# Gated attention and mixture of experts: the dense expert behind the last tile, eight tiles loaded right behind the table

## What is computed

```python
x = x + tanh(g_xattn) * (0.6 * sigmoid(si[:, :, None] + sj[:, None, :] + b) + 0.4 * layernorm(x))
xf = layernorm(x).reshape(-1, 256)
scores = sigmoid(xf @ w_router)                 # 1024 x 32
# the 4 best of 8 groups by (scores + corr_bias), and of their experts the 6 best
combine = zeros.at[token, topk_idx].add(scores[topk_idx])
eo = einsum('etm,emh->eth', silu(xf @ gate_w[e]) * (xf @ up_w[e]), down_w)
routed = einsum('te,eth->th', combine, eo)
shared = silu(xf @ sh_gate_w) * (xf @ sh_up_w) @ sh_down_w
out = x + tanh(g_ffn) * (routed + shared)
```

## Time and profile before

| | |
|---|---|
| median of three runs | 255.59 us (254.35 to 256.19) |
| span of the profiled execution | 256.1 us, from the first to the last instruction |
| TensorE products / weight loads | 220.1 us (86%) / 172.2 us (67%) |
| VectorE / ScalarE / POOL | 130.3 (51%) / 79.8 (31%) / 147.0 (57%) us |
| tiles | 56, in 7 rounds of eight |
| mean transfer rate | 208 GB/s |

### The profile page before, as it was taken

The page is one execution under the profiler, slowest core; times in us unless marked ns, Lnnn a source line. Parts: engine busy times, 40 slices in busy tenths (PEclk is TensorE's granted clock), DMA queues, the critical chain, the costliest instruction groups (busy, mean ns, idle before and its releaser), DMA issues.

```text
span 256.1 us, 5045 instructions
## 1 busy us (share of the span) xinstructions
PE 220.1 (86%) x1043; PEld 172.2 (67%) x1044; DVE 130.3 (51%) x528; ACT 79.8 (31%) x222; POOL 147.0 (57%) x139
## 2 busy tenths in 40 slices
PE   6896899996899986999999999999999998996000
PEld 5886687884667754877787777778777776774000
DVE  2598768989545542434444534444443443443344
ACT  3607022020011222343434344344444433433000
POOL 6226557777777742564675657656575665465500
PEclk9659599999799999999999999999999999999555
DMA  6999999999999989899785658767677675357787
GB/s 194 274 295 275 408 405 332 243 327 331 320 355 337 385 230 359 179 230 238 140 144 104 114 95 161 115 117 116 103 123 107 113 109 89 42 62 139 157 215 248
DMA packets 41016, 53.32 MB, mean 208 GB/s; under 512 B 5134, under 2 KB 35438, under 8 KB 40998
## 3 DMA queue, kind: packets, MB, share of 16 engines
q1 hardware_dynamic: 24944, 30.40, 40.3%
q0 software_dynamic: 11280, 17.99, 35.5%
q10 hardware_dynamic: 4774, 4.74, 7.1%
HBM read 31.72 MB, written 21.40 MB: 207 GB/s over the span
## 4 chain that ended last, share of the span: by engine, by line
PE 69%; DVE 13%; DMA 11%; issue 3%; POOL 1%; ACTq 1%; ACT 1%; SPq 0%; POOLq 0%
PE pG L734 25%; PE pY L748 17%; PE pG L673 5%; PE pX L728 5%; DMA sum_dram<-xnT,idx 5%; PE pH L742 4%; PE pG L757 4%; DMA xg<-rows_dram 3%; PE pY L684 3%; PE pY L776 3%; DMA given<-in_L_xattn_b_dram 2%; DMA wgu<-sum_dram 2%; PE pX L614 1%; DVE xs L900 1%; DVE rows L894 1%
## 5 line engine op out<-in xcount | busy, mean ns | idle before, releaser
L435 POOL DMA_INDIRECT sum_dram<-xnT,idx x56 | 87.1, 1556 | 61.6 <-ACT xnT L549 36.3
L734 PE MATMUL pG<-wgu,sdown 128*128 x224 | 76.1, 462 | 1.6 <-issue 1.1
L423 POOL DMA_INDIRECT rows_dram<-rows,row_i x48 | 47.2, 983 | 19.0 <-issue 13.8
L748 PE MATMUL pY<-wd,sup 88*128 x224 | 57.5, 379 | 0.0
L1122 DVE COPY sup<-pH 88x256 f32<-88x256 f32 x56 | 23.5, 420 | 58.0 <-PE pH L742 58.0
L734 PEld LDWEIGHTS pG<-wgu,sdown 128*128 128x128 f32 x224 | 38.4, 191 | 14.6 <-issue 2.6
L549 ACT ACTIVATE xnT<-pY,wt 128x256 f32<-128x256 f32 x56 | 26.6, 474 | 57.2 <-PE pY L748 24.7
L748 PEld LDWEIGHTS pY<-wd,sup 88*128 88x128 f32 x224 | 38.0, 190 | 3.2 <-issue 0.2
L742 PEld LDWEIGHTS pH<-ident,sgate 128*88 128x88 f32 x112 | 17.8, 161 | 13.6 <-issue 0.5
L542 ACT ACTIVATE sgate<-pG 128x176 f32<-128x176 f32 x56 | 17.8, 317 | 25.1 <-PE pG L734 24.6
L537 ACT ACTIVATE sdown<-pX 128x256 f32<-128x256 f32 x56 | 21.0, 377 | 7.4 <-PE pX L728 4.5
(11 more groups left out here) (181 smaller groups left out, 236.3 us busy)
## 6 DMA issues: line engine op xcount, KB each, us to landing
wgu<-in_L_ffn_gate_w_dram SPq DMA_DIRECT2D x8, 704.0 KB, 11.0
wgu<-in_L_ffn_up_w_dram SPq DMA_DIRECT2D x8, 704.0 KB, 11.7
wd<-in_L_ffn_down_w_dram SPq DMA_DIRECT2D x8, 640.0 KB
sum_dram<-zeros POOLq DMA_DIRECT2D x3, 1152.0 KB, 13.6
wgu<-sum_dram SPq DMA_DIRECT2D x12, 256.0 KB, 3.9
rows<-rows_dram ACTq DMA_DIRECT2D x16, 144.5 KB, 4.2
xg<-rows_dram ACTq DMA_DIRECT2D x16, 144.5 KB, 3.7
rows_dram<-zeros SPq DMA_DIRECT2D x8, 289.0 KB, 4.7
```

The costliest lines, as they stand in the source:

```text
L423: pool.indirect_dma_start(rows_dram[:, :], bass.IndirectOffsetOnAxis(ap=row_i[:, j, k:k + 1], axis=0), rows[:, j, :], None).then_inc(done, 16)
L435: pool.indirect_dma_start(sums_dram[into[s]][:, :], bass.IndirectOffsetOnAxis(ap=idx[:, s:s + 1], axis=0), y[s], None, compute_op=ALU.add) ...
L734: ins = nc.tensor.matmul(pG[par][:, 0:2 * M].rearrange("t (g m) -> t g m", g=2), xT[:, par, k, :], wgu[:, bass.ds(e, 1), :, k, :].rearrang ...
L748: ins = nc.tensor.matmul(pY[par][:, 0:H], hT[0:MI, par, i, :], wd[:, bass.ds(e, 1), i, :], start=(i == 0), stop=(i == I - 1))
```

## The change

The dense expert's weights are no longer read apart; it uses those in `wgu` and `wd`, and its products follow the last tile's. There, ScalarE copies the transposed h. ScalarE issues the loads of tiles 0 to 7 right behind the table and the first 24 scatters, and FETCH is new. `xnT` lives to the end; y has eight places of its own in scratch tiles of the choice and of the table, which are now cut from two large ones (`choice`, `table`). The wait for the last 24 scatters moves from POOL to SP, ahead of its wait for the last batch of weights. The sums are read into six places in `rows` and `xg_own`; the seventh read and those behind it wait until VectorE has added what was there. `weigh_busy` moves behind `shared_gate(11)`. `added(i, n)` names the semaphore and value of the n-th addition of round i, as before.

```diff
-XRING = 8
+XRING = ROUND
 YRING = ROUND
...
-    FETCH = {t: max((t - 5) // 2, t - XRING + 1) for t in range(5, HELD * ROUND)}
+    FETCH = {t: 9 if 12 <= t < 16 else t - XRING + (2 if t >= 16 else 1) for t in range(XRING, HELD * ROUND)}
...
-        y = [xnT[:, k, s * H:(s + 1) * H] for k in range(K) for s in range(T // H)]
-
-        busy_gu = xg_own[:, :, :].rearrange("p i c -> p (i c)")[:, 0:2 * K * M].rearrange("p (g k m) -> p g k m", g=2, k=K)
-        busy_d = wd[:, E - BATCH, :, :]
-        not_busy, is_busy, busy_key = (cur[:, i, :] for i in range(SEGS))
+        y = [of[:, i * H:(i + 1) * H] for of, n in ((choice, 5), (table, YRING - 5)) for i in range(n)]
...
+        parts = [of[:, :, :].rearrange("p j c -> p (j c)")[:, i * HALVES * H:(i + 1) * HALVES * H].rearrange("p (j c) -> p j c", c=H)
+                 for of, n in ((rows, J * ROW // (HALVES * H)), (xg_own, JH * ROW // (HALVES * H))) for i in range(n)]
...
-                    if i == 7:
-                        sp.wait_ge(s_by, J)
...
-                if i == PICKED:
-                    weights_of_busy()
...
+            sp.wait_ge(s_rest, REST)
+            sp.sem_inc(s_placed, 1)
             sp.wait_ge(s_const, 3)
             for n in range(24 - FLOW, 24):
                 weights_there(n)
...
-            for i in LEFT:
-                for s in [s for s in range(ROUND) if INTO_LAST[s] == i]:
-                    sp.wait_ge(s_add[s], (last + 1) * 16)
+            sp.wait_ge(s_taken, last * ROUND + ROUND)
+            sp.sem_inc(s_passed, 1)
+            for n, i in enumerate(LEFT):
+                for s in [s for s in range(ROUND) if INTO_LAST[s] == i][-2:]:
+                    sp.wait_ge(*added(last, s))
                     sp.sem_inc(s_passed, 1)
                 for b in range(B):
-                    js = slice(b * HALVES, (b + 1) * HALVES)
-                    sp.dma_start(sums[i][:, js, :],
-                                 sums_dram[i][0:T, :].rearrange("(j p) c -> p j c", p=P)[:, js, :]).then_inc(s_sums[i][b], 16)
+                    part = n * B + b
+                    if part >= len(parts):
+                        sp.wait_ge(s_summed, part - len(parts) + 1)
+                    sp.dma_start(parts[part % len(parts)],
+                                 sums_dram[i][0:T, :].rearrange("(j p) c -> p j c", p=P)[:, b * HALVES:(b + 1) * HALVES, :]
+                                 ).then_inc(s_sums[i][b], 16)
             for b in range(B):
-                sp.wait_ge(s_fin, b + 1)
+                sp.wait_ge(s_summed, (SUMS - 1) * B + b + 1)
                 sp.dma_start(out_rows[:, b * HALVES:(b + 1) * HALVES, :],
                              xs[:, b * HALVES:(b + 1) * HALVES, :]).then_inc(s_out, 16)
...
-            pool.wait_ge(s_rest, REST)
-            pool.sem_inc(s_placed, 1)
             for t in range(ROUND):
                 add(t, t, 0)
...
-            def silu_busy(j):
...
-
-            silu_busy(0)
+                if reused or s >= YRING:
+                    act.wait_ge(*added(i, s - YRING))
+                nc.scalar.activation(y[s % YRING], pY[s % 2][:, 0:H], ACT.Copy, scale=wt[:, s:s + 1]).then_inc(s_yc, 1)
+
             act.wait_ge(s_tiles, 1)
-            for j in range(1, J):
-                silu_busy(j)
-                if j == 1:
-                    act.wait_ge(s_scat, 16 * JH * TOPK)
-                if j <= JH:
-                    load(act, j - 1, j - 1)
+            act.wait_ge(s_scat, 16 * JH * TOPK)
+            for t in range(XRING):
+                load(act, t, t)
             copy_xT(0, 0)
             copy_xT(1, 1)
-            load(act, JH, JH)
             silu(0, 0)
 
...
                 turn(last, s, ROUND - s)
+
+            def silu_common(j):
+                act.wait_ge(s_cgu, j + 1)
+                nc.scalar.activation(sg[:, j % 2, :], pG[j % 2][:, 0:M], ACT.Silu).then_inc(s_csilu, 1)
+
+            def copy_hT_common(j):
+                act.wait_ge(s_chT, j + 1)
+                nc.scalar.activation(hT[0:MI, j % 2, :, :].rearrange("p i t -> p (i t)"), pH[j % 2][0:MI, 0:I * P],
+                                     ACT.Copy).then_inc(s_chTc, 1)
+
+            silu_common(0)
             scale_y(last * ROUND + (ROUND - 1), ROUND - 1, True, last)
+            for j in range(J):
+                if j + 1 < J:
+                    silu_common(j + 1)
+                copy_hT_common(j)
...
-            pe.wait_ge(s_busyw, 64)
-            gate_up_busy(0)
-            for j in range(J):
-                if j + 1 < J:
-                    gate_up_busy(j + 1)
-                turn_h_busy(j)
-                if j:
-                    down_busy(j - 1)
             pe.wait_ge(s_tiles, 1)
             transpose_x(0, 1, 0)
             transpose_x(1, 1, 1)
-            down_busy(J - 1)
             e_first = look_up(0)
             pe.wait_ge(s_ready, e_first + 1)
             gate_up(0, 0, e_first)
...
                         if first and t <= 2:
-                            pe.wait_ge(s_byc, J - 2 + t)
...
+                    ins = nc.tensor.matmul(pG[j % 2][:, 0:2 * M].rearrange("t (g m) -> t g m", g=2),
+                                           xnT[:, k, j * P:(j + 1) * P],
+                                           wgu[:, bass.ds(e_common, 1), :, k, :].rearrange("p e g m -> p (e g) m"),
+                                           start=(k == 0), stop=(k == K - 1))
+                ins.then_inc(s_cgu, 1)
+
+            def turn_h_common(j):
+                pe.wait_ge(s_ch, j + 1)
+                for i in range(I):
+                    ins = nc.tensor.transpose(pH[j % 2][0:MI, i * P:(i + 1) * P],
+                                              h[:, j % 2, :].rearrange("t (p i) -> t i p", i=I)[:, i, :], ident[:, :])
...
+                    pe.wait_ge(s_cyc, j - 1)
+                for i in range(I):
+                    ins = nc.tensor.matmul(pY[j % 2][:, 0:H], hT[0:MI, j % 2, i, :], wd[:, bass.ds(e_common, 1), i, :],
+                                           start=(i == 0), stop=(i == I - 1))
+                ins.then_inc(s_cy, 1)
+
+            e_common = pe.value_load(busy_i[0:1, 0:1], min_val=0, max_val=E - 1)
+            gate_up_common(0)
             pe.wait_ge(s_hTc, last * ROUND + ROUND)
             pe.wait_ge(s_yc, last * ROUND + (ROUND - 2))
             down(last * ROUND + (ROUND - 1), (ROUND - 1) % 2, e_last)
+            for j in range(J):
+                if j + 1 < J:
+                    gate_up_common(j + 1)
+                turn_h_common(j)
+                if j:
+                    down_common(j - 1)
+            down_common(J - 1)
 
         @block.vector
         def _(dve):
...
-            weigh_busy()
...
             shared_gate(11)
+            weigh_busy()
             dve.wait_ge(s_tableT, 1)
             V.tensor_copy(tiles[:, :], tiles_bank).then_inc(s_tiles, 1)
...
-            gate_busy(0)
-            for j in range(J):
-                copy_hT_busy(j)
-                if j + 1 < J:
-                    gate_busy(j + 1)
-                if j:
-                    add_busy(j - 1)
-            add_busy(J - 1)
             take(0, 0, 0, used=False)
             gate(0, 0)
...
+            def gate_common(j):
+                dve.wait_ge(s_csilu, j + 1)
+                V.tensor_tensor(h[:, j % 2, :], sg[:, j % 2, :], pG[j % 2][:, M:2 * M], ALU.mult).then_inc(s_ch, 1)
+
+            def add_common(j, summed):
+                dve.wait_ge(s_cy, j + 1)
+                if summed:
+                    dve.wait_ge(s_summed, summed)
+                V.scalar_tensor_tensor(xs[:, j, :], pY[j % 2][:, 0:H], busy_w[:, j:j + 1], xs[:, j, :],
+                                       op0=ALU.mult, op1=ALU.add).then_inc(s_cyc, 1)
+
+            def add_sum(n, bs, ready):
+
+                dve.wait_ge(s_cyc, ready)
+                if n:
+                    dve.wait_ge(s_summed, n * B)
+                for b in bs:
                     js = slice(b * HALVES, (b + 1) * HALVES)
-                    dve.wait_ge(s_sums[i][b], 16)
-                    ins = V.tensor_tensor(xs[:, js, :], xs[:, js, :], sums[i][:, js, :], ALU.add)
-                    if i == LEFT[-1]:
-                        ins.then_inc(s_fin, 1)
+                    dve.wait_ge(s_sums[LEFT[n]][b], 16)
+                    V.tensor_tensor(xs[:, js, :], xs[:, js, :], parts[(n * B + b) % len(parts)], ALU.add).then_inc(s_summed, 1)
+
+            gate_common(0)
+            dve.wait_ge(s_shyc, J)
+            for j in range(J):
+                if j + 1 < J:
+                    gate_common(j + 1)
+                if j:
+                    add_common(j - 1, (j - 1) // 3 * B)
+                if j in (3, 6):
+                    add_sum(j // 3 - 1, range(B), j)
+            add_sum(SUMS - 1, range(B - 1), J - 1)
+            add_common(J - 1, (SUMS - 1) * B)
+            add_sum(SUMS - 1, range(B - 1, B), J)
```

More of the change, by code:

```diff
@@ L1 @@
+import itertools
 import math
@@ L201, in gated_xattn_moe @@
         sfc = comb
```

(28 more changed lines are left out.)

114 lines of the change are left out of this document (26 added, 88 removed).

## The result

Over four executions of each kernel the changed one took 263.93 us (263.02 to 264.45) and the one before 255.69 us, a ratio of 1.032 [1.028, 1.036]: slower by 8 us. The forecast was 255.9 us, its range ended at 259.6, and slower had the smallest chance. The profiled execution took 263.85 us at a span of 262.0; the span of before was 256.1. In the runs of this study the time stands 1.8 to 1.9 us above the span, so the profiled execution of before, of which only the span is known, was probably a longer one than its median.

The account below looks back on a forecast made before the run. TensorE's own work and a 21.3 us tail of transfers waiting for each other were taken as the bound. Last tile's down product 4.95 earlier, tail 5.2 longer: span 256.35, forecast 255.9 us, range 251.0 to 259.6.

Parts of the forecast that it names:

- Waits moved between queues: SP's wait for the last scatters lands by 100.25, tile 9 due 102.2: hidden by 2 us; weights cost 0.
- The new S0: Start of tile 0's first gate/up product (S4: tile 4's, and so on): 79.65 instead of 89.05, gain 9.4 us.
- The early stalls: TensorE's waits for late loads of tiles 4 and 5 vanish; S4 - S0 falls from 12.13 to 8.13, gain 4.0 us.
- the cold clock: Lower TensorE clock at tile 0's start, behind the longer gap: loss of 2.0 us, bounds 0 and 3.
- Tile 12: Load held back to turn 9 comes late: TensorE stands 4.65 us ahead of its transposes, plus 1.8 for the clock.
- The tail: From the last tile's down product to the end: 26.5 us against 21.3, VectorE setting the pace; a loss of 5.2.
- The sum: Whole span: 256.1 - 4.95 + 5.2 = 256.35 us; forecast time 255.9 us.
- The slower one: Rival: the four loads from tile 12 collide, landing after 7.7 us, and tail reads take 5.4; 260.1 us, chance 0.22.
- The faster one: Rival: tile 12's load lands in 2.6 us, stall 2.75 without clock loss; 252.2 us, chance 0.34 with what lies near.
- It doesn't do what it says: Rival: an early tile needs second-half rows, ScalarE stands until 100.25, start some 12 us later; about 270 us, chance 0.02.
- a gap before tile 9 (SP's wait): Sign against the forecast: TensorE idle ahead of tile 9 because SP's wait for the last scatters delays its weights report.

Follow-up runs that it names:

- e4_flow5: Changed kernel with five parts of weights in flight instead of three; 264.22 us, 1.033 of the kernel before.
- e1_ready: Changed kernel, but TensorE asks for weights batch by batch in the second round of eight too, for all only ahead of the third; 259.12 us, 1.012.
- e7_pause: Changed kernel, but SP again stands ahead of the fourth weight batch until the dense expert is known; 263.01 us, 1.022.
- e5_spread: e3_both with VectorE's twelve additions of the sums spread over the dense blocks instead of standing in fours; 249.43 us, 0.972.
- e2_fetch: Changed kernel, but from tile 12 on loads are issued one a turn, five tiles ahead, instead of 12 to 15 together at turn 9; 259.67 us, 1.005.
- e9_all: e5_spread plus 38 identity products on TensorE filling the gap ahead of tile 0's first gate/up product; 250.01 us, 0.972 of the kernel before.
- e3b_both: Second run of e3_both, the same kernel, as base for later runs; 252.47 us, 0.979 of the kernel before.
- e3_both: Changed kernel with the edits of e1_ready and e2_fetch together; 251.89 us, 0.984 of the kernel before.
- e8_order: Changed kernel, but SP waits for the last 24 scatters behind its reports on the last weights; 265.98 us, 1.030 of the kernel before.

## Why the prediction was wrong

**The step that failed** stands under "Waits moved between queues". It took the wait ahead of tile 9 to be SP's new wait for the scatters, "Hidden by 2 us", and closed the weights with "the weights come earlier, and TensorE did not wait for them before: 0". The first half was right: the scatters' wait ended near 97.2, well within the 100.25 given. The second half took it that a wait which had cost nothing never would. Its slack was to be read: the report at 104 in the kernel before against a tile 9 that the forecast's own sum moved to 102.2. That alone made a hole of some 2 us, to which TensorE's own work behind the report (1.13 us) and the clock (2.6) would come. It measured 6.3 us instead of 0: 3.74 of lateness and 2.58 of clock. The sentence "beyond that each us costs one" had the mechanism in hand, for the wrong transfer.

**The new S0** was right in its chain: eight loads issued in a row by ScalarE from 69.03 to 78.57, S0 10.2 us behind the first of them (forecast 10.3: 79.65 less 69.35). That the sum hit, 79.24 against 79.65, is luck in good part: the 24th scatter went out at 60.82 and not at 62.15, and the first load followed it by 8.21 us and not by 7.2 (6.2 + 1.0), two errors that cancel. In the kernels with the same front the 24th scatter goes out between 57.42 and 60.82, the first load between 64.96 and 69.03, and S0 comes between 75.55 and 79.24. In e4_flow5 it came at 81.14, since tile 1's load landed 8.84 us behind its issue, where the forecast took 7.7 for the slowest. And in the changed kernel a second wait ends at S0: ScalarE's first copy is done at 79.00, but the profile names SP's report on a batch of weights, at 79.15 (L279), as the last releaser. The product follows the copy by the same 0.24 us as in e1_ready, so the report cost nothing; a later one would have, and the forecast has no term for it. In the changed kernel an earlier start is lost again at tile 9: in e7_pause S8 comes at 97.89, 2.5 us earlier, and S9 at 105.82, 0.8 earlier. **The early stalls and the cold clock**: S4 came at 90.38 against 89.8. S4 - S0 is 11.14 where the forecast had 8.13 and 2.0 for the clock: the cold start cost 3.0, the end of its bounds.

**Tile 12** was right in its mechanism and nearly in its size, 6.8 against 6.45, though by errors that cancel. The load was issued at S10 + 2.9, not 2.4, and landed after 3.4 us, not 4.5. And a term was missing: behind the stall S11 starts 1.09 us behind the transposes ahead of it, where 0.23 is usual. The profile calls 0.58 us of it "issue"; ScalarE copies nothing between 112.3 and 120.67. In the program TensorE reads the tile's expert into a register there; that this is what shows is a reading, not tested. Ahead of S9 it is likewise: for its 1.06 us the profile names ScalarE's copy at 105.58, but that is tile 10's, which the product of tile 9 doesn't need. The Trainium skill, DMA: Bandwidth & Descriptors, section "Anatomy of one DMA — SWDGE (gpsimd) path", from whose fit the prediction drew an estimate of 2.3 us for such a load, is on transfers that GpSimd issues; this one is issued by ScalarE. The trace has 3.4 here, with the guard rows in flight, 1.1 more.

**The tail** was right: 25.7 against 26.5, VectorE without a gap behind the last dense blocks, the reads of the sums in time and the scatter-adds hidden. e5_spread confirms that VectorE was its limit.

**The sum.** 256.35 was forecast and 262.0 measured: tile 9 +6.32, S4 +0.60, tile 12 +0.31, the small stalls that went and the tiles behind them -0.72, the tail -0.84, together +5.65 but for rounding. The rest of the 8.0 us by which the time missed is the last step: the forecast took 0.45 off its span of 256.35, while in the runs of this study the time stands 1.85 above the span (263.85 and 262.0), 2.3 more.

**The rivals.** None named the mechanism. The slower one came nearest in time, 260.1, through loads that land after 7.7 us, and it was wrong: they landed after 3.4. The faster one had tile 12 cheap; e2_fetch, where it costs nothing, still takes 1.005 of the kernel before and not the 0.987 of that rival (252.2 to 255.59), since the hole at tile 9 stays. The last one ("It doesn't do what it says") had a wrong sum: passing at 100.25, with a chain of 11.3 us behind it, gives a start at 111.5, which is 22.5 us later than before and not 12, and so a time above 280 us and not 270. It did not happen: the first eight loads went out in a row. What would show the forecast wrong did list "a gap before tile 9 (SP's wait)", for another releaser. The range was too narrow above, since it took no account of a second wait with a known arrival.

## What to carry to other kernels

When work is moved away from ahead of a stage, list every wait of that stage with the time at which its releaser comes in the old trace, and compare each with the new due time, those above all that cost nothing before: the weights here, with the 16 engines at a share of 1.0 up to 100 us, did not follow a stage that starts 10 us earlier, and a wait for "everything" is to be cut to what the next step needs. Here both such waits had to go: taken away alone neither made the kernel faster than before (1.012 and 1.005), together they did (0.984 and 0.979). With the additions of the tail spread as well, e5_spread takes 249.43 us, 0.972 of the kernel before; e9_all has the same ratio, and no kernel here a lower one.

## What the runs showed of the hardware that was not expected

- The last weight part reports late. The share of the transfer engines falls to 0.50 at 100 us and to 0.11 at 101, and the part (704 KB) lands only at 103.8. In the kernel before the share fell to 0.28 from 102 to 103, and the guards behind the report went out at 104.08. What the part waits for in those 3 us no row shows.
- The start of the tiles differs by up to 3.7 us between executions of kernels with the same front, and already the issue of the 24th scatter by 3.4 us (above). So does the time at which the weights are all there: the guards behind their report start at 100.36, 101.72, 102.27 and 106.82 in e3b_both, e3_both, e5_spread and e2_fetch, which have the same loads of tiles. In e8_order it is 110.24, though its edit stands behind the last weights and can't delay them. Why is open, so the width of the hole at tile 9 (2.2 us ahead of the transposes in the changed kernel, 4.2 in e7_pause, 8.4 in e2_fetch) hangs on the execution and not on the edit alone.
- Five parts in flight instead of three stretched a part's landing from 11.95 to 18.4 us and brought the end forward by 1 us.
- A hole in TensorE's work cost its length and more: behind 3.3 us without products ahead of S9 (2.24 + 1.06) the clock stood at 0.50 from 106 to 112, a loss of 2.58 us. Behind the 1.3 us of e3b_both, which lie in three pieces, the products took 1.45 us where 1.35 is usual.
